# Delta-rule output in a fused transformer kernel: who scales the mapped rows and who adds them to the residual

## The reference, cut to what matters

```python
q, k, v = silu(x @ Wq), silu(x @ Wk), silu(x @ Wv)      # 16 heads of 8
...
out = dplr_delta_rule(q, k, v, a, gk).reshape(b, n, d)  # a recurrence over the 512 rows
out = out * sigmoid(x @ Wg1 @ Wg2)                      # gate
mu, var = mean(out), mean((out - mu) ** 2)              # over the 128 numbers of a row
out = (out - mu) * rsqrt(var + 1e-05) * norm_w
return out @ Wo                                         # added to x by the caller
```

## Time and profile before

| | us |
|---|---|
| median of 3 runs | 1160.75 |
| the runs | 1152.72, 1160.75, 1161.76 |
| the profiled execution's own time | 1149.88 |
| its span from the first to the last instruction | 1148.0 |
| start of the first moments(u) of the output | 931.35 |
| first instruction of the expert layer behind it | 956.80 |

### The profile page before, as it was taken

One profiled execution on the slowest core, in us unless ns is written; L12 is line 12 of the kernel. 1 busy time (PEld: TensorE's weight loads), 2 busy tenths in 40 slices (PEclk: granted clock), 3 DMA queues, 4 the chain that ended last, 5 costly groups with the idle time before them and its releaser, 6 DMA issues. The chain is left out here.

```text
span 1148.0 us, 26589 instructions
## 1 busy us (share of the span) xinstructions
PE 837.9 (73%) x9317; PEld 622.0 (54%) x9317; DVE 744.4 (65%) x1688; ACT 535.1 (47%) x1207; POOL 557.9 (49%) x691
## 2 busy tenths in 40 slices
PE   3788878788888452999188999467678674619992
PEld 2455555556556351888025785155556564518881
DVE  7567767767667650232364899999999997512224
ACT  4568767767767111544055220355555530205450
POOL 3466666765665352454450010277777832523542
PEclk9989999989889555999688999779988895559997
DMA  5243144234140115676338400000020110155775
GB/s 159 79 154 124 59 132 138 61 116 146 40 129 3 55 40 147 172 209 176 97 65 110 64 1 1 0 1 0 0 73 0 37 37 12 41 151 154 203 195 165
DMA packets 129207, 101.80 MB, mean 89 GB/s; under 512 B 20640, under 2 KB 116832, under 8 KB 129056
## 3 DMA queue, kind: packets, MB, share of 16 engines
q1 hardware_dynamic: 122384, 89.38, 29.0%
q0 software_dynamic: 5120, 10.53, 2.6%
q10 hardware_dynamic: 1600, 0.49, 0.2%
HBM read 57.98 MB, written 35.45 MB: 81 GB/s over the span
## 5 line engine op out<-in xcount | busy, mean ns | idle before, releaser
L679 DVE TENSOR_SCALAR a_mag<-a_pS 128x1024 int32<-128x1024 int32 (+1 forms) x192 | 178.2, 948 | 70.3 <-PE a_pS L879 64.4
L461 ACT ACTIVATE a_pw<-a_mag,a_eps_a 128x1024 f32<-128x1024 f32 (+1 forms) x192 | 173.0, 933 | 52.1 <-DVE a_mag L679 50.4
L1192 POOL DMA_INDIRECT ys_dram<-f_yo,f_who x96 | 91.9, 957 | 137.4 <-DVE f_yo L1472 120.7
L343 POOL TENSOR_TENSOR a_pw<-a_pw,a_decay 128x256 f32<-128x256 f32 x128 | 93.0, 728 | 95.0 <-ACT a_pw L461 94.5
L879 PE MATMUL a_pS<-a_qf,a_kf 64*64 64x192 bf16 (+3 forms) x1536 | 107.9, 264 | 17.6 <-DVE a_mag L679 13.9
L2393 PE MATMUL d_c<-d_pb_p,ident 128*128 128x256 f32 x256 | 73.4, 457 | 46.2 <-POOL d_pb_p L1876 46.2
L1254 ACT ACTIVATE f_hs<-f_bH,f_bs 128x256 f32<-128x256 f32 x192 | 75.4, 475 | 64.4 <-PE f_bH L1572 64.1
L1457 DVE TENSOR_SCALAR f_ysT<-f_bY,f_bs 128x256 f32<-128x256 f32 x48 | 23.2, 484 | 116.3 <-PE f_bY L1582 116.3
L1572 PE MATMUL f_bH<-f_xsT,f_w1s 128*128 128x256 f32 x384 | 93.8, 388 | 0.0
L2393 PEld LDWEIGHTS d_c<-d_pb_p,ident 128*128 128x128 f32 x256 | 59.4, 236 | 60.6 <-issue 44.9
L1582 PE MATMUL f_bY<-f_hs,f_w2s 128*128 128x256 f32 x384 | 90.8, 379 | 0.0
(11 more groups left out here) (359 smaller groups left out, 1778.9 us busy)
## 6 DMA issues: line engine op xcount, KB each, us to landing
parts_scratch<-a_parts SPq DMA_DIRECT2D x32, 384.0 KB, 3.5
f_w1s<-in_L_ffn_w_dram SPq DMA_DIRECT2D x48, 256.0 KB, 2.8
f_w2s<-in_L_ffn_w_dram SPq DMA_DIRECT2D x48, 256.0 KB, 3.1
a_kf<-parts_scratch SPq DMA_DIRECT2D x16, 512.0 KB, 5.4
a_qf<-parts_scratch SPq DMA_DIRECT2D x16, 512.0 KB, 6.5
f_xs<-xs_dram SPq DMA_DIRECT2D x48, 129.0 KB, 2.3
parts_scratch<-a_parts SPq DMA_DIRECT2D x16, 256.0 KB, 2.5
xs_dram<-blank SPq DMA_DIRECT2D x24, 129.0 KB, 2.9
```

The costliest lines, as they stand in the source:

```text
L343: pool.tensor_tensor(own, own, decay[:, k, m, hf:NP:2, :], ALU.mult)\
L461: act.activation(pw[:, n % 4, 0:N], mag[:, n % 3, 0:N], ACT.Square, bias=eps_a[:, 0:1])\
L679: dve.tensor_scalar(mag[:, n % 3, 0:2 * N].bitcast(I32).rearrange("p (l t) -> p l t", l=2), pS[:, 2 * (n % 2):2 * (n % 2) + 2, 0:N].bitcas ...
L1192: pool.indirect_dma_start(ys_dram[f][:, :], bass.IndirectOffsetOnAxis(ap=who[:, q, a:a + 1], axis=0), yo[:, q, a, :], None).then_inc(ys_ou ...
```

## The change

VectorE keeps the moments and the reciprocal (now `inverse(u)`). The four instructions L2271 of a unit are gone. ScalarE makes four Copy activations with the inverse deviation as the scale of each partition, from the PSUM bank to `mapped`, a view of two halves on the tile `W`, each half four tiles wide. GpSimd adds one half to the four tiles of `x` in a single instruction. `ost_done`, for which TensorE's matmuls of unit u + 3 wait, is now given by ScalarE after its four copies. ScalarE's order is spread(0), then spread(u) and scaled(u - 1) for u = 1 to 7, then scaled(7), where `spread` is the Sqrt. A half of `mapped` is written again when GpSimd has added it. VectorE waits for GpSimd's last add before the block ends. The diff, cut:

```diff
+        mapped = W[:, :, :, :].rearrange("p d j c -> p (d j c)")[:, 0:8 * C].rearrange("p (a k c) -> p a k c", a=2, k=4)
...
         @block.gpsimd
...
+            for u, (i, h) in enumerate(UNITS):
+                pool.wait_ge(s["ost_done"], u + 1)
+                four = x[:, TT * 4 * h:TT * 4 * (h + 1), :].rearrange("p (b i) c -> p i b c", i=TT)[:, i]
+                pool.tensor_tensor(four, four, mapped[:, u % 2], ALU.add).then_inc(row_odd, 1)
...
         @block.scalar
...
-            for u in range(len(UNITS)):
+            def spread(u):
                 act.wait_ge(s["ost_step"], u + 1)
                 act.activation(ors[:, 0, 4 * u:4 * u + 4], omv[:, 4 * u:4 * u + 4, 1], ACT.Sqrt,
                                bias=eps_ln[:, 0:1]).then_inc(s["o_sqrt"], 1)
+            def scaled(u):
+                act.wait_ge(s["oy_ps"], u + 1)
+                act.wait_ge(s["o_rstd"], u + 1)
+                if u >= 2:
+                    act.wait_ge(row_odd, row_odd_0 + B + u - 1)
+                for k in range(4):
+                    ins = act.activation(mapped[:, u % 2, k, :], mapped_in[u % 3][:, P * k:P * k + P], ACT.Copy,
+                                         scale=ors[:, 1, 4 * u + k:4 * u + k + 1])
+                ins.then_inc(s["ost_done"], 1)
+            spread(0)
+            for u in range(1, len(UNITS)):
+                spread(u)
+                scaled(u - 1)
+            scaled(len(UNITS) - 1)
...
         @block.vector
...
-            def add_in(u):
-                i, h = UNITS[u]
-                yp = mapped_in[u % 3]
+            def inverse(u):
                 at = slice(4 * u, 4 * u + 4)
                 dve.wait_ge(s["o_sqrt"], u + 1)
                 dve.reciprocal(ors[:, 1, at], ors[:, 0, at]).then_inc(s["o_rstd"], 1)
-                dve.wait_ge(s["oy_ps"], u + 1)
-                dve.wait_ge(s["o_rstd"], u + 1)
-                for k in range(4):
-                    j = TT * (4 * h + k) + i
-                    ins = dve.scalar_tensor_tensor(x[:, j, :], yp[:, P * k:P * k + P], ors[:, 1, 4 * u + k:4 * u + k + 1],
-                                                   x[:, j, :], ALU.mult, ALU.add)
-                ins.then_inc(s["ost_done"], 1)
...
                 moments(u)
-                add_in(u - 1)
-            add_in(len(UNITS) - 1)
+                inverse(u - 1)
+            inverse(len(UNITS) - 1)
+            dve.wait_ge(row_odd, row_odd_0 + B + len(UNITS))
```

## The result

The changed kernel has a median of 1151.47 us (22 runs, 1142.89 to 1155.19) against 1156.63 for the kernel before (22 runs, 1146.11 to 1161.76). The ratio is 0.9953, 95% interval 0.9933 to 0.9973: by it 5.4 us less (by the medians 5.2), clear of noise, and within the 1% that I had called no change. A second measurement gave 0.9978 (0.9947 to 1.0008), which by itself would not tell a gain from none.

What follows compares the result with a forecast made beforehand. VectorE was taken to bound the delta rule's output. 5.6 us at the gating plus 1.8 in the last two units, less 1.6 holding and 1.5 tail, gave 4.3 less: 1156.5 us, range 1148 to 1162.

Steps and rivals of the forecast that it cites:

- VectorE as the path, and 5.6 us at the gating: Delta rule's output: VectorE is the path, units fall from 2.50 to 1.45 us, gating of `ob_c` starts 5.6 us earlier.
- ScalarE's copies at 1.15: ScalarE's four scaled copies of a unit take 1.15 us, bounds 1.11 and 1.57.
- GpSimd's add at 1.26: GpSimd's single add of a unit's four tiles takes 1.26 us.
- the upper bound of 1.45: Most that GpSimd's add of a unit should take: 727 ns for 256 columns, doubled to 1.45 us.
- Holding at the gating, 1.6: VectorE's two gating instructions for `ob_c`, reading two on-chip inputs, are held by GpSimd's adds, costing 1.6 us.
- The last two units gain 1.8, since they no longer wait for TensorE: Units 6 and 7, behind the gating: TensorE's clock stays high and VectorE no longer waits for it, 1.8 us less.
- Tail 4.4: From the last moments to the next layer: 4.4 us, 1.5 more than before, as ScalarE's copies and GpSimd's adds follow.
- Sum 4.3: Whole output: next layer begins at 952.5 instead of 956.8, 4.3 us less.
- Holding of all that VectorE reads on chip: Rival, chance 0.08: GpSimd's adds hold aggregates and reciprocals too, units cost 2.62 us, next layer 1.8 later, 1162.5 us.
- table loads: Rival, chance 0.03: Sqrt and scaled Copy need different ScalarE tables, two loads of 1.28 us a unit, 10 later, 1171 us.
- The rival of less gain: Chance 0.17: copies 1.57 us, both gatings held, TensorE at the lower clock; the 4.3 us gain vanishes, 1160.7 us.
- my 1156.5: Forecast median time of the changed kernel in us: the median before less 4.3.

Runs made afterwards that it cites:

- the probes: Changed kernel plus a small unused VectorE product of two on-chip inputs (128x4) behind each reciprocal; output stretch 21.9 us, against 25.4 in the kernel before with the same products.
- the run with the adds behind the gating: Changed kernel with eight places in `mapped`, GpSimd's adds from unit 3 on waiting until VectorE has gated `ob_c`; output stretch 19.7 us.
- The half of the change: Against the changed kernel: ScalarE scales into eight places, VectorE adds each unit in one instruction, GpSimd does nothing; output stretch 22.5 us.
- the run with the added idle time: Changed kernel with two unused VectorE reductions ahead of the gating of `ob_c`, leaving TensorE idle longer; output stretch 23.7 us.
- the run with doubled adds: Changed kernel with a second, unused GpSimd add of each unit into a spare tile; output stretch 28.0 us.

## Why the prediction was right, step by step

The time alone proves little: the range of 1148 to 1162 also holds the kernel before (1156.63), so no change at all would have met it. What bears the mechanism out is the stretch, term by term.

- **VectorE as the path, and 5.6 us at the gating.** Measured 5.55. The single units were not all 1.45: they took 1.28, 1.25, 1.81, 1.34 and 1.28 (942.04 to 949.00, a mean of 1.39). VectorE's own unit is 1.25 and not 1.36, because the next moments begin 0.06 after the reciprocal does, for which the prediction says 0.10 in one place and 0.15 in the sum. The 1.81 comes from one wait for TensorE, behind ScalarE's first copies; the prediction had TensorE and ScalarE as limits in every unit. Both errors were small and of opposite sign, so that the 5.6 is met so closely is in part luck.
- **ScalarE's copies at 1.15.** Measured 1.12 to 1.14. The estimate from a group of four with a pointer was good. No table load came between Sqrt and Copy.
- **GpSimd's add at 1.26.** Median 1266 ns, with 1.66 and 1.72 us for the two beside the gating, which the upper bound of 1.45 did not cover: I had thought of VectorE held by GpSimd and not of the reverse.
- **Holding at the gating, 1.6.** Right in kind, shown by the adds moved away and by the probes; the gating grew by 1.06, and only 0.77 of it reached the last moments, as the run with the adds behind the gating shows. GpSimd's add came 0.13 after the first product and not just ahead of it, so one product was held and not one and a part.
- **The last two units gain 1.8, since they no longer wait for TensorE.** Without the holding, 5.76 fell to 4.05 (the run with the adds behind the gating), so 1.71. The prediction puts this down to the clock; the rows of the kernel before show that L2271 stood ahead of moments(7) as well, and that most of the gain needs both gone.
- **Tail 4.4.** Measured 4.58; the difference is the block's end: 0.54 from the end of the last add (957.84) to the next layer, and not 0.32. The half of the change, where VectorE makes the last add, has 0.54 there too, so it does not come from GpSimd being last; why it is longer is open.
- **Sum 4.3.** 4.86 in the stretch, and 5.4 by the ratio, whose interval reaches from 3.1 to 7.7. By the terms as measured it is 5.55 + 1.71 - 0.77 - 1.65 = 4.84. The term that was mis-sized is the holding, by 0.8 on the path; the tail (by 0.15) and the last two units (by 0.1) took some of it back.
- **The rivals.** Holding of all that VectorE reads on chip is refuted by reciprocals of 0.15 beside adds, table loads by their absence. The rival of less gain had TensorE's lower clock as one of its terms, at 1.3 us; the run with the added idle time shows that the term exists and puts it at 1.7.

The median before, 1160.75 of three runs, became 1156.63 of 22, and the changed kernel's 1151.47 lies 5 below my 1156.5 mostly for that reason (4.1 of the 5.0).

## What to carry to other kernels

Before work goes to GpSimd, list what VectorE does beside it. Here products of two on-chip inputs waited for GpSimd's running add, at 128x4 as at 128x512, and the large ones slowed it in turn (1.66 and 1.72 us in place of 1.27), while the moments on PSUM (0.86 to 0.89) and reciprocals (0.15) did not wait. Moving work down a chain of engines shortens each unit and lengthens the drain: give the last units back to the engine that has the shortest way to the end (worth 1.67 us here). A gain of 5 in 1150 us is not seen in two spans (1148.0 and 1148.3 here); measure the stretch between two events that both kernels have.

## What was not expected of the hardware

- The holding is mutual: adds of 1266 ns took 1.66 us and 1715 ns beside the gating, and up to 1716 in the run with doubled adds, where both products were held (1270 and 1753 ns).
- TensorE's clock does not follow from the idle time alone. After 2.43 us without work (half of the change) it was at 1.2 GHz and the transposes took 1.12; after 2.50 us in the run with probes they took 0.66 at 2.4 GHz, but there the clock fell just behind them: the matmuls at 953.65 took 1.46 in place of 1.06 and the next transposes 1.06, as at 1.2 GHz. After 3.75 and 4.45 us they took 1.11. What TensorE did before differs between them, and this was not taken apart. So the changed kernel's high clock at the end, after 1.14 us of idle time, was forecast rightly, but from one earlier case and not from a rule.
